# Second of four graph networks: degree factors moved through the relu, sides packed into parts of TensorE, steps overlapped

## The reference, cut to what matters

```python
def _gcn_norm(edge_index, n_nodes):      # self loops are added to the edges
    deg = segment_sum(ones, dst)
    deg_inv_sqrt = where(deg > 0, rsqrt(deg), 0.0)
    return src, dst, deg_inv_sqrt[src] * deg_inv_sqrt[dst]

def _gcn_conv(x, src, dst, norm, W, b, n_nodes):
    h = x @ W
    msg = h[src] * norm[:, None]
    return segment_sum(msg, dst, n_nodes) + b

h = relu(_gcn_conv(x, src, dst, norm, W1, b1, n))
h = relu(_gcn_conv(h, src, dst, norm, W2, b2, n))
h = relu(_gcn_conv(h, src, dst, norm, W3, b3, n))
```

## Time and profile before

| | us |
|---|---|
| median of 3 runs (lowest, highest) | 8515.5 (8512.02, 8523.6) |
| profiled execution, its own time | 8527.12 |
| its span | 8525.3 |
| PE busy | 5690.7 (67%) |
| DVE busy | 4696.7 (55%) |
| POOL busy | 3350.0 (39%) |
| ACT busy | 2495.5 (29%) |

### The profile page before, as it was taken

One profiled execution on the slowest core, in us unless ns is written; L12 is line 12 of the kernel. 1 busy time (PEld: TensorE's weight loads), 2 busy tenths in 40 slices (PEclk: granted clock), 3 DMA queues, 4 the chain that ended last, 5 costly groups with the idle time before them and its releaser, 6 DMA issues.

```text
span 8525.3 us, 71449 instructions
## 1 busy us (share of the span) xinstructions
PE 5690.7 (67%) x21484; PEld 2626.3 (31%) x21492; DVE 4696.7 (55%) x6891; ACT 2495.5 (29%) x4074; POOL 3350.0 (39%) x3658
## 2 busy tenths in 40 slices
PE   2997894431488745576766667675675799999950
PEld 1434442221243311222222222223354444444420
DVE  5563332232444466686867778684375556666640
ACT  1663331110132211111111111112321266666630
POOL 3777745565433333343434353445406200000026
PEclk9997886655799867787878888787797899999975
DMA  2004557896543478797978788796203100000000
GB/s 77 11 9 142 196 207 88 74 78 53 92 91 64 83 237 249 207 264 209 258 214 255 233 231 263 207 266 82 33 1 26 15 10 15 13 15 15 9 18 19
DMA packets 535938, 986.79 MB, mean 116 GB/s; under 512 B 99055, under 2 KB 288259, under 8 KB 535172
## 3 DMA queue, kind: packets, MB, share of 16 engines
q1 hardware_dynamic: 424900, 911.36, 29.8%
q0 software_dynamic: 110656, 70.87, 18.3%
HBM read 778.66 MB, written 203.60 MB: 115 GB/s over the span
## 4 chain that ended last, share of the span: by engine, by line
PE 37%; DMA 18%; POOL 15%; issue 13%; DVE 11%; ACT 5%; SPq 1%; POOLq 0%; DVEq 0%; ACTq 0%
POOL gathered L787 9%; DMA gathered<-table,idx_slot 6%; DMA blocks<-net 5%; PE ps L917 5%; PE ps L1305 4%; DMA ring<-net 4%; PE ps L979 4%; POOL pair_slot L787 2%; PE ps L1067 2%; DVE ring L2093 2%; PE ps L1068 2%; POOL last_of L802 2%; POOL out_dram L901 1%; PE ps L1072 1%; PE ps L1412 1%
## 5 line engine op out<-in xcount | busy, mean ns | idle before, releaser
L787 POOL DMA_INDIRECT gathered<-table,idx_slot x2156 | 2099.4, 974 | 1583.0 <-DVE ring L2093 880.7
L2093 DVE TENSOR_TENSOR ring<-ring,ps 128x1024 f32<-128x1024 f32 (+2 forms) x1008 | 1073.0, 1083 | 499.3 <-DMA ring<-net 464.6
L979 PE MATMUL ps<-ring,mats 128*32 128x512 f32 (+2 forms) x4032 | 709.5, 657 | 372.6 <-DVE ring L2093 311.9
L917 PE MATMUL ps<-mats,gathered 128*128 128x128 f32 x1029 | 217.3, 343 | 1051.1 <-DMA gathered<-table,idx_slot 1001.2
L896 POOL COPY idx_slot<-idx_run_end 128x16 int32<-128x16 int32 (+2 forms) x14 | 2.7, 195 | 1556.3 <-SPq L769 1538.5
L917 PE MATMUL ps<-mats,w 128*128 128x128 f32 x1323 | 279.1, 354 | 449.8 <-DVE w L2556 249.9
L917 PEld LDWEIGHTS ps<-mats,gathered 128*128 128x128 f32 x1029 | 146.5, 171 | 1221.0 <-DMA gathered<-table,idx_slot 1087.9
L780 POOL COPY idx_slot<-idx_row 128x16 int32<-128x16 int32 (+2 forms) x154 | 33.6, 218 | 1085.4 <-SPq L548 1040.5
L2160 DVE SCALAR_TENSOR_TENSOR x_block<-ps,bias,blocks 128x512 f32<-128x512 f32 x300 | 224.7, 749 | 384.3 <-PE ps L1072 384.1
L979 PEld LDWEIGHTS ps<-ring,mats 128*32 128x32 f32 x4032 | 156.0, 125 | 873.4 <-issue 542.4
L2093 DVE TENSOR_TENSOR blocks<-blocks,ps 128x1024 f32<-128x1024 f32 (+2 forms) x336 | 357.4, 1085 | 62.8 <-DMA blocks<-net 58.2
(11 more groups left out here) (279 smaller groups left out, 12241.8 us busy)
## 6 DMA issues: line engine op xcount, KB each, us to landing
ring<-net SPq DMA_DIRECT2D x792, 512.0 KB
blocks<-net SPq DMA_DIRECT2D x264, 512.0 KB
net<-ring SPq DMA_DIRECT2D x176, 512.0 KB, 2.8
table<-w SPq DMA_DIRECT2D x165, 256.0 KB, 2.9
gathered<-table,idx_slot POOLq DMA_INDIRECT x2352, 3.4
ring<-net SPq DMA_DIRECT2D x144, 256.0 KB
x_sp<-x_block SPq DMA_DIRECT2D x79, 256.0 KB, 8.4
x_block<-x_sp SPq DMA_DIRECT2D x79, 256.0 KB, 5.4
```

Of the source, the lines that this page charges most:

```text
L787: pool.indirect_dma_start(dests(k), None, rows, bass.IndirectOffsetOnAxis(ap=dst[:, k:k + 1], axis=0)).then_inc(done, 16)
L917: last = nc.tensor.transpose(dst[:, k * P:k * P + P], src[:, k * P:k * P + P], mat["ident"])
L979: last = mm(message[t * D:t * D + D, 0:wd(i)], adders[2 * m + c], ring[slot][:, c * wd(i):(c + 1) * wd(i)], start=(m == 0 and c == 0), sto ...
L2093: v.tensor_tensor(pair, pair, state, ALU.mult).then_inc(sig["pr"][S_], 1)
```

## The change

The factor d of a node is positive, so d·relu(W x + b) = relu(W (d x) + b d). The change uses this in T3 and P4, and reorders both.

- Setup: the factor d of each slot's destination, one number for each of the 196 tiles of 128 slots and each partition, is made once (`edge_deg`, a Sqrt on ACT and a reciprocal on DVE over 196 columns, in the stage `ENDS`), and a tile `b1_rows` holds the bias b1 in one row for each quarter (a memset, four copies of one column, a transpose on PE and a copy).
- P3 and T3: P3 leaves d·(d·sum) in `h`, one multiplication more for each side. The sweep of quarter 0 is done inside P3, one or two blocks behind; T3 keeps three sweeps. W1's product takes only the 32 rows of its quarter, and the spread product is replaced by `b1_rows` times the degree row, added in the same bank. The relu has no bias and DVE no multiplication. The copy out of PSUM becomes one ACT instruction for each 128 columns, with the slot's degree factor as a scale for each partition.
- P4: for each block DVE makes d·state and d·d ahead (four passes, `degrees`). In each step the D side works on quarter (t+1) mod 4 while the S side works on t, so the W1 products and the bias products of the two sides use different rows of TensorE, and the W3 products different output columns. DVE does one pass for each side and step (`join`). W2's product follows one step later and W3's two steps later, over block ends too. The D rows are loaded in that order, and the degree rows into three buffers in turn.

```diff
-    add("P3", "head c1a g", alternate="ld_gs")
+    add("P3", "head c1a lin g", alternate="ld_gs")
...
+        deg_state = [[ring[2 + k][:, u * WB:u * WB + WB] for u in SPACES] for k in (0, 1)]
+        deg_square = [[blocks4[:, 2 * k + u, :] for u in SPACES] for k in (0, 1)]
+        conv_first, conv_joined = [w[1], w[2]], [w[3], w[4]]
+        conv_second = [[ring[4 + k][:, u * WB:u * WB + WB] for u in SPACES] for k in (0, 1)]
...
# PE, P3 and T3
+            def products(t, i):
+                par, n = i % 2, q.n("b4", i % 2, i // 2, t * halves(EB)[i % 2])
+                rows = quarter_rows(t)
+                pe.wait_ge(sig["b4"][par], n + CREDIT)
...
+                mm(fit(pA[par], i), wts[rows, WEIGHTS.index(f"w1_{t}"), :], h[S_][rows, col(i)], start=True, stop=False)
+                mm(fit(pA[par], i), b1_rows[rows, :], fit(degrees, i)[rows, :], start=False, stop=True).then_inc(sig["b1"][par], 1)
+                mm(fit(pC[par], i), spread_bf[:, t, :], blk(keep, i), start=True, stop=True).then_inc(sig["bk"][par], 1)
...
             for i in range(EB):
-                early_head(q, i, "c1a")
...
+                light_head(i)
+                if i:
+                    products(0, i - 1)
+                if i > 1:
+                    wide_rows(0, i - 2)
...
+            for t in range(1, T):
+                products(t, 0)
+                for i in range(EB):
+                    if i + 1 < EB:
+                        products(t, i + 1)
+                    wide_rows(t, i)
...
# PE, P4
+            def wide_in(i, t):
...
+                for u in SPACES:
+                    pe.wait_ge(sig["q3"][u], q.n("q3", u, i, t) + CREDIT)
                     turn(fit(pA[u], i), G[t % 2][u], q_of(i)).then_inc(sig["q_head"][u], 1)
...
+            def first_layer(i, t):
+                for u in SPACES:
+                    rows = quarter_rows(side_quarter(u, t))
...
+                    mm(fit(pB[u], i), wts[rows, WEIGHTS.index(f"w1_{side_quarter(u, t)}"), :], fit(deg_state[i % 2][u], i)[rows, :],
+                       start=True, stop=False)
+                for u in SPACES:
...
+                    mm(fit(pB[u], i), b1_rows[quarter_rows(side_quarter(u, t)), :], fit(deg_square[i % 2][u], i)[rows, :],
+                       start=False, stop=True).then_inc(sig["q1"][u], 1)
...
+            def third_layer(i, t):
+                for u in SPACES:
+                    pe.wait_ge(sig["q6"][u], q.n("q6", u, i, t) + 1 + CREDIT)
                     if t == 0:
...
+                        pe.wait_ge(sig["g"][u], q.n("g", u, i) + CREDIT)
+                for u in SPACES:
+                    cols = quarter_rows(side_quarter(u, t))
+                    mm(fit(pD[u], i)[cols, :], wts[:, WEIGHTS.index(f"w3_{side_quarter(u, t)}"), cols], fit(conv_second[t % 2][u], i),
+                       start=True, stop=True).then_inc(sig["q7"][u], 1)
+
+            steps = [(i, t) for i in range(EB) for t in range(T)]
+            for n, (i, t) in enumerate(steps):
+                wide_in(i, t)
+                first_layer(i, t)
+                if n > 0:
+                    second_layer(*steps[n - 1])
+                if n > 1:
+                    third_layer(*steps[n - 2])
...
# ACT, T3 and setup
+            f(edge_deg, edge_deg, ACT.Sqrt, bias=one_col("one")).then_inc(s_aset, 1)
...
-                    f(fit(w[4][par], i), fit(pD[par], i), ACT.Copy).then_inc(sig["b4"][par], 1)
+                    for k in range(q_of(i)):
+                        at = tb(i) + k * T + t
+                        last = f(w[4][par][:, k * P:k * P + P], pD[par][:, k * P:k * P + P], ACT.Copy, scale=ends[:, at, 1:2])
+                    last.then_inc(sig["b4"][par], 1)
...
# DVE, P4
+            for i in range(EB):
                 for t in range(T):
...
+                    join(i, t)
+                    if t == 1 and i + 1 < EB:
+                        degrees(i + 1)
+                    if t == 2 and i:
+                        third_out(i - 1)
```

More of the change, by code:

```diff
@@ L214, in plan @@
     add_tab("T2")
-    add("P3", "head c1a g", alternate="ld_gs")
+    add("P3", "head c1a lin g", alternate="ld_gs")
     two_buffers("P3", "ld_d")
     n4 = tuple(T * h for h in halves(EB))
-    add("T3", "ld_d4 b1 b1r bd bk bm b3 b3t b4 st_tab4", blocks=n4)
-    add("P4", "ld_d g q_head q1 q1r qd q2 q3 q4 q5 q6 q7", s="scan", times=Q4, alternate="ld_gd", wide=True)
+    add("T3", "b1 b1r bk b3 b3t b4 st_tab4", blocks=n4)
+    for par in (0, 1):
+        out["T3"].use(before, "ld_d4", par, 1, (T - 1) * halves(EB)[par])
+    add("P4", "ld_d c1a g q_head q1 q1r q3 q5 q6 q7", s="scan", times=Q4, alternate="ld_gd", wide=True)
     add_tab("T4")
@@ L1359, in _ @@
             tables("T2", "P2")
-            q = p_["P3"]
-            for i in range(EB):
-                early_head(q, i, "c1a")
[L1366 to L1387, removed]
@@ new lines, in wide_rows @@
+            def wide_rows(t, i):
+                par = i % 2
+                pe.wait_ge(sig["b3"][par], q.n("b3", par, i // 2, t * halves(EB)[par]) + 1 + CREDIT)
+                turn(fit(pD[par], i), w[3][par], q_of(i)).then_inc(sig["b3t"][par], 1)
+            for i in range(EB):
+                light_head(i)
+                if i:
+                    products(0, i - 1)
+                if i > 1:
+                    wide_rows(0, i - 2)
+            products(0, EB - 1)
+            for i in (EB - 2, EB - 1):
+                wide_rows(0, i)
@@ L2323, in _ @@
             last.then_inc(s_set, 1)
+            v.memset(w[4][1][:, 0:P], 0.0).then_inc(s_end4, 1)
+            dve.wait_ge(s_end4, 2)
+            for t in range(T):
+                last = v.tensor_copy(w[4][1][:, t * D:t * D + 1], one_col("b1"))
+            last.then_inc(s_set, 1)
+            dve.wait_ge(s_set, 18)
+            dve.wait_ge(s_pset, 6)
+            v.tensor_copy(b1_rows, pC[1][:, 0:P]).then_inc(s_set, 1)
             tables("T_setup", None)
@@ L2333, in _ @@
             settle(dve)
+            dve.wait_ge(s_aset, 1)
+            v.reciprocal(edge_deg, edge_deg).then_inc(s_set, 1)
             def body(i, par, j, q=q):
@@ new lines, in _, with degrees @@
+            for t in range(1, T):
+                for i in range(EB):
+                    wide_sums(t, i)
+            q = p_["P4"]
+            def degrees(i):
+                for u in SPACES:
+                    deg = fit(d_turn[i % 3][u], i)
+                    landed(dve, "ld_d", u, q.n("ld_d", u, i))
+                    if i > 1:
+                        dve.wait_ge(sig["q1"][u], q.n("q1", u, i - 1) + CREDIT)
+                    v.tensor_tensor(fit(deg_state[i % 2][u], i), blk(h[u], i), deg, ALU.mult)
+                    v.tensor_tensor(fit(deg_square[i % 2][u], i), deg, deg, ALU.mult).then_inc(sig["c1a"][u], 1)
@@ L2463, in _ @@
+            degrees(0)
+            for i in range(EB):
+                for t in range(T):
+                    join(i, t)
[3 more added lines that the diff above has]
+                        third_out(i - 1)
+            third_out(EB - 1)
             tables("T4", "P4")
```

221 lines of the change are left out of this document (114 added, 107 removed).

## The result

| | before | after |
|---|---|---|
| median | 8519.55 us (4 runs, 8512.0 to 8524.9) | 8435.66 us (4 runs, 8430.5 to 8441.9) |
| ratio after / before | | 0.9898, 95% interval 0.988 to 0.9915 |
| profiled execution, its span | 8527.1, 8525.3 us | 8430.5, 8428.7 us |

The change saves 84 us of the 200 that were forecast. The time lies above the range.

The account below looks back on a forecast made before the run. PE's products bound P4, the loop of products, transposes and ACT's copy T3, POOL's gathers P3. P4 -170 and -15, P3/T3 -18, setup +3.5 sum to -199.5 us: 8316 us median, range 8280 to 8366.

Parts of the forecast that it names:

- P4's full blocks: P4: step 5.85 us, 1.5 us wait a block, block 24.9 us, eleven 274 instead of 443.9 us: -170 us.
- A: P4: POOL sets the pace, block 20.86 to 22 us, 38 us less than forecast, 8278 us; chance 0.12.
- B: P4: two sides' W1 products don't overlap, step 0.85 us longer, 8358 us; 8442 if neither bias nor W3 overlap; chance 0.12.
- C: P4: granted clock falls part of the time, 0.8 instead of 0.97, +55 us, 8371 us; chance 0.07.
- P4's small blocks: P4: 12 steps in 62.1 us before, 42.5 us after plus 4.5 for draining: -15 us.
- T3's copy: T3: four scaled ACT copies take 1.18 us instead of 0.60, +0.58 us a full block.
- T3's period: T3: same products (bias for spread), only the copy longer, period 3.9 us; T3 155.1 instead of 172.8 us, -18.
- Rival D: P4 and T3: 32-row products keep PE at 1.2 GHz, T3 +76 on -18, total 8659 us; chance 0.02.
- P3 and setup: P3 stays at 267 us; setup's Sqrt, reciprocal and bias tile cost +3.5 us, between 0 and 6.
- E: P3: PE's products between gathers' transposes delay blocks, 1 us each, 14 us, 8330 us; chance 0.67 together with the forecast.

Follow-up runs that it names:

- the experiment without pairs: Changed kernel with its output copy moved, D side of P4's edge steps on the same quarter as S: 9297.64 us (one run), against 9145.88 with pairs.

## Why the prediction was wrong

- **P4's full blocks**: the time after was right. Step 5.84 for 5.85, the wait 1.4 for 1.5, block 24.79 for 24.9, eleven of them 275.5 for 274; the first step ran at the low level and took 8.6 us. The time before was misread: 443.9 us held 8.3 us of the last block, so the saving is 160, not 170. Rivals A, B and C did not happen there; the experiment without pairs shows what B's mechanism costs in full.
- **P4's small blocks**: -12.8 for -15 is luck. They took 57.6 us instead of 47, and the time before was 70.4 and not 62.1 by the same misread cut. Of the 10.6 us, 3.9 are the wait ahead of the first full block, for rows that GpSimd gathers. Another 3.8 are in the last block, whose four steps took 18.2 us for 14.4. The head ran at a mean clock of 0.65 where it had 0.86 before. That is not T3's low level carried over: with full rows in T3, TensorE took 35.0 us (2435.1 to 2470.1, first occasion) and 33.7 us (2401.0 to 2434.7, third) for the same two blocks, against 34.3 here.
- **T3's copy**: right, 1.14 for 1.18 us; ACT's relu is hidden as forecast. The Trainium skill's figures (ScalarE: Activation LUTs, What ACT_TABLE_LOAD costs) made it an estimated 1.26; the trace does not agree, and stands nearer to the row.
- **T3's period: the step that failed.** "Their period holds the same products (bias for spread)" took the products at the durations of the earlier trace rows. They were the same in count and columns, but had 32 rows instead of 128, and the stage ran at 1.2 GHz: 6.40 us instead of 3.90, T3 +72.3 instead of -18. These are 90 of the 103 us of error. That the rows are the cause is shown by the edits of rows alone, in both directions; another 10 us are the misread cut.
- **Rival D** had this mechanism, with a price in T3 of 33 x 2.3 = +76 on -18, close to what came. What was wrong was to tie it to P4: its point of decision was the clock in P4, and its chance of 0.02 rested on PE being busy 80% there. The stage with the worse product mix was T3, where nothing is paired, and it deserved a rival of its own: 8316 + 76 gives 8392.
- **P3 and setup**: +5.6 for +3.5 agrees by luck. The 3.5 were for setup, which cost some 0.7 us: POOL was 1.5 us ahead of the kernel before in front of the new Sqrt and reciprocal (658.10 for 659.64) and 0.9 ahead behind them (710.55 for 711.42), and P3's first copy of indices still came earlier, at 1962.4 us for 1963.5. Of P3's growth 4.5 us are one idle stretch of POOL between two gathers, 10.0 us instead of 5.5 (up to 2158.24 and 2154.99 us), which the profile gives no cause for. The blocks before it are 20.9 us apart in both kernels, so E did not happen in them.

The full-row version of T3 keeps what the forecast had counted on: -173 to -169 us. Its ratio of 0.979 to the kernel before against 0.990 makes it about 1% faster than the changed kernel, though the two were not run side by side.

## What to carry to other kernels

Putting a product on a part of TensorE's rows pays where two of them run at once. Where it stands alone it saves nothing (at the high level the W1 product on 32 rows of the old T3 took 1.05 us to the next group, 2331.94 to 2332.99, against 0.96 on 128), and here it cost the clock: read the granted clock of each stage after such an edit, not only of the stage that was meant. In a stage like T3, which waits on TensorE and was at the high level, full-row products were the faster choice, even with three quarters of their rows zero.

## What the hardware showed

- The granted clock did not follow TensorE's busy share. 0.50 with 29.7 of 30 us busy (32-row products added), 0.87 with 388 of 392 busy (P4 unpaired), 1.00 with 40.3 of 60 busy (T3 full rows).
- In the old T3, products on 64 rows gave the same level, 0.50, and the same period to 0.01 us, 5.86, as on 32 (5.85).
- Four more bf16 products of 32 rows a block cost nothing in T3 at the low level, where TensorE had a wait of 1.23 us to put them in (period 6.40 with and without); four of 128 rows cost 0.4 us (2341.10 to 2347.90, 6.80).
- Added useless full-row work made the kernel faster than its 32-row control: 8369 us (4 runs) against 8434 (one run), on the same occasion.
